# Projection bias on GpSimd, matmul operands on two byte phases, and new engine orders

## The chip, the cores and the metric

The kernel runs on one core of one Trainium2 chip. The metric is device time in microseconds (us). One execution was also taken by the hardware profiler. TensorE is PE in the rows (PEld is its weight load), VectorE is DVE, ScalarE is ACT, GpSimd is POOL, and SP is the engine that issues the DMAs.

## The reference

Two layers on x of shape (2, 1024, 256), all in float32, cut to what matters here:

```python
# layer 0: cross attention to a context of 154 rows, a router over 3 experts, a gate
nx = layer_norm(x)
weights = softmax(nx @ Wq @ (context @ Wk).T / 16)           # one head
evidence = weights @ (context @ Wv)
combined = concat([nx, evidence, anchor])                      # anchor: cond, the same in every row
probs = softmax(combined @ router_W + router_b)
routed = sum_e probs[e] * (silu(combined @ e_w1[e] + e_b1[e]) @ e_w2[e] + e_b2[e])
g = sigmoid(silu(combined @ gate_w1 + gate_b1) @ gate_w2 + gate_b2)
x = x + g * (routed @ out_w + out_b)
# layer 1: cross attention with 16 heads of 16 to the same context, modulated by cond
xq, xkv = ada_ln(x, cond), ada_ln(context, cond)
q, k, v = xq @ Wq + bq, split(xkv @ Wkv + bkv)
out = softmax(q @ k.T / 4) @ v                                  # per head
return x + (out @ Wp + bp)                                      # bp: the bias that the change moves
```

## The kernel before

The 2048 tokens are cut into 8 tiles `t` of 256 (two halves `s` of 128). `LAST` is tile 7 and `NEXT` is tile 6. Each engine's work is written out by hand as a list of steps in `ORDERS`, and each engine goes through its own list in order; a step is `name.tile.part`. A step waits on semaphores for the steps of other engines that it needs. TensorE's list has 545 steps.

A float32 product is made of three float32r matmuls (helper `exact`, L1658 to L1660): high by high, low by high, high by low. In `mm(out, left, right)`, `left` is the stationary operand (loaded with LDWEIGHTS) and `right` is the moving one. The steps on TensorE that matter here:

- `za.t.u` and `z.t.u` (`hidden_half`, L1658 to L1660 and L1878): the two halves of hidden unit `u` (7 units a tile: the gate's first layer and the three experts' in slices of 256). 13 matmuls a half: the stationary operands are the weights WNh, WNl, VWh, VWl, VWD (`hidden_w_*`, `context_w_*`), the moving ones NXh, NXl, PTh, PTl, PTD (`normed_*`, `probs_T_*`). Over the kernel that is 8 x 7 x 2 x 13 = 1,456 matmuls.
- `p.t.u` (`second`): the second layer of unit `u`. 12 matmuls: stationary SH and SL (`hidden_high`, `hidden_low`), moving W2h, W2l, GWh, GWl (`expert_out_*`, `gate_out_*`). Over the kernel 8 x 7 x 12 = 672. SH is made by ScalarE (L1023) and SL by GpSimd (step `h`, L1592).
- `query.t`: 12 matmuls, stationary `query_w_*`, moving `query_in_*`. `most` (L1997) and `score` (L2027): attention scores, with `query_stack` and `pair_keys`, whose column offsets differ from step to step. `value` (L2050, L2053): in four column groups of 32.
- `proj.t` (`proj_part`; for the last tile `lead.7`, `last.0`, `last.1`): for each half `s`, four matmuls L2061 (stationary `outs_low`, moving `proj_w_high`), two L2065 (`outs_pairs`, `proj_w_low`) and, behind the first of them, one L2063 (`bias_rows` by `second_bias`) that adds bp, which is kept as a high and a low row in `second_bias`.
- `cv.0`, `warm.0`, `ck.0`, `cv.1`, `fold.0`: the start. `cv.0` waits for the first DMA; `warm.0` is 4 matmuls on zeros (8 rows in the trace) and waits only for a memset on VectorE. `fill` are matmuls on data that nobody reads, between the waits at the end.

VectorE subtracts the projection's PSUM bank from the token tile X (`proj`, `last_add`), and SP stores X. X has 5 slots, with a reload for later tiles. `xhat.t` on ScalarE reads X for the second layer norm.

SBUF places are given out by `put`, one after the other, each size rounded up to 32 bytes; `run` lays overlays on top of places given out before. No place is aligned to more than that.

Of the kernel before, what the change touches and what calls it, by code (L numbers as in the profile page):

```python
# [89 lines left out]
def packed(np, v):  # L90
# [35 lines left out]
    gate_rows[[1, 17]] = v["L1_xcond_bp"]  # L126
# [138 lines left out]
        most.1.14 z.3.0 za.3.1 most.1.15 vw.1.0 z.3.1 vw.1.1 row.1.0 p.2.5 p.2.6 proj.0 za.3.2 z.3.2 vw.1.2 score.1.0 p.3.0 qx.2 score.1.1 za.3.4 score.1.2
        score.1.3 za.3.3 score.1.4 score.1.5 score.1.6 query.2 z.3.3 score.1.7 value.1.0 value.1.1 att.4 score.1.8 score.1.9 z.3.4 most.2.0 most.2.1 p.3.1
        most.2.2 score.1.10 p.3.2 za.3.5 most.2.3 most.2.4 score.1.11 value.1.2 value.1.3 most.2.5 most.2.6 z.3.5 most.2.7 most.2.8 za.3.6 prob.4 most.2.9
        most.2.10 z.3.6 p.3.3 vw.1.3 most.2.11 p.3.4 za.4.0 most.2.12 most.2.13 vw.1.4 z.4.0 za.4.1 most.2.14 z.4.1 most.2.15 vw.1.5 p.3.5 row.2.0 p.3.6
        vw.1.6 za.4.2 z.4.2 norm.5 p.4.0 proj.1 score.2.0 za.4.3 qx.3 z.4.3 score.2.1 score.2.2 score.2.3 p.4.1 score.2.4 query.3 score.2.5 score.2.6
        score.2.7 value.2.0 value.2.1 score.2.8 score.2.9 att.5 score.2.10 score.2.11 value.2.2 most.3.0 most.3.1 value.2.3 most.3.2 most.3.3 za.4.4 most.3.4  # L270
        za.4.5 z.4.4 most.3.5 most.3.6 p.4.2 prob.5 z.4.5 most.3.7 most.3.8 p.4.3 za.4.6 most.3.9 z.4.6 p.4.4 za.5.0 most.3.10 most.3.11 z.5.0 za.5.1 p.4.5
        most.3.12 p.4.6 za.5.2 most.3.13 most.3.14 most.3.15 z.5.1 z.5.2 row.3.0 norm.6 proj.2 p.5.0 za.5.3 qx.4 score.3.0 score.3.1 z.5.3 score.3.2 score.3.3
        score.3.4 query.4 score.3.5 score.3.6 score.3.7 value.3.0 value.3.1 score.3.8 att.6 score.3.9 za.5.4 p.5.1 score.3.10 p.5.2 most.4.0 score.3.11
        most.4.1 za.5.5 most.4.2 most.4.3 most.4.4 z.5.4 most.4.5 most.4.6 value.3.2 value.3.3 most.4.7 most.4.8 za.5.6 most.4.9 most.4.10 prob.6 z.5.5
        most.4.11 most.4.12 p.5.3 most.4.13 most.4.14 z.5.6 most.4.15 p.5.4 za.6.0 z.6.0 row.4.0 za.6.1 norm.7 z.6.1 p.5.5 p.5.6 proj.3 score.4.0 score.4.1
        score.4.2 p.6.0 score.4.3 score.4.4 score.4.5 za.6.2 score.4.6 za.6.3 qx.5 score.4.7 value.4.0 value.4.1 score.4.8 query.5 score.4.9 score.4.10 z.6.2
        z.6.3 score.4.11 att.7 value.4.2 value.4.3 most.5.0 most.5.1 most.5.2 p.6.1 za.6.4 most.5.3 z.6.4 most.5.4 most.5.5 za.6.5 most.5.6 most.5.7 p.6.2
        most.5.8 prob.7 most.5.9 z.6.5 most.5.10 za.6.6 most.5.11 p.6.3 z.6.6 p.6.4 most.5.12 most.5.13 most.5.14 za.7.0 z.7.0 p.6.5 p.6.6 most.5.15 za.7.1
        za.7.2 z.7.1 row.5.0 z.7.2 p.7.0 za.7.3 qx.6 proj.4 score.5.0 score.5.1 score.5.2 query.6 score.5.3 score.5.4 z.7.3 score.5.5 p.7.1 value.5.0
        score.5.6 score.5.7 score.5.8 value.5.1 score.5.9 score.5.10 most.6.0 p.7.2 most.6.1 score.5.11 most.6.2 value.5.2 most.6.3 most.6.4 most.6.5  # L280
        value.5.3 most.6.6 most.6.7 most.6.8 za.7.4 most.6.9 most.6.10 z.7.4 most.6.11 za.7.5 p.7.3 za.7.6 z.7.5 z.7.6 most.6.12 most.6.13 most.6.14 p.7.4
        most.6.15 row.6.0 p.7.5 p.7.6 proj.5 score.6.0 score.6.1 fill.0 score.6.2 score.6.3 fill.1 score.6.4 fill.2 score.6.5 score.6.6 value.6.0 score.6.7
        qx.7 score.6.8 value.6.1 score.6.9 query.7 score.6.10 value.6.2 score.6.11 most.7.0 most.7.1 most.7.2 most.7.3 most.7.4 most.7.5 most.7.6 most.7.7
        most.7.8 most.7.9 most.7.10 most.7.11 most.7.12 most.7.13 row.7.0 value.6.3 most.7.14 most.7.15 score.7.0 score.7.1 score.7.2 score.7.3 score.7.4
# [57 lines left out]
        load.0 late.0 late.1 key.0 key.1 stack.0.0 stack.0.1 stack.0.2 stack.0.3 row.0.0 stack.1.0 again.0 stack.1.1 stack.1.2 stack.1.3 again.1 again.2  # L342
        row.1.0 proj.0 again.3 reload.0 stack.2.0 stack.2.1 stack.2.2 stack.2.3 again.4 again.5 again.6 row.2.0 proj.1 reload.1 stack.3.0 stack.3.1 stack.3.2
        stack.3.3 row.3.0 proj.2 reload.2 stack.4.0 stack.4.1 stack.4.2 stack.4.3 row.4.0 stack.5.0 stack.5.1 proj.3 stack.5.2 stack.5.3 row.5.0 stack.6.0
        stack.6.1 stack.6.2 proj.4 stack.6.3 unstack.0 row.6.0 stack.7.0 proj.5 stack.7.1 stack.7.2 stack.7.3 proj.6 last.0 last.1
# [1776 lines left out]
```

## Time and profile before

| what | value |
|---|---|
| median of 3 runs | 431.21 us (428.57, 431.21, 814.35) |
| the profiled execution | 429.68 us, of which the span of its instructions is 427.9 us |
| TensorE busy | 416.2 us (97%) |
| VectorE, ScalarE, GpSimd busy | 327.5, 225.6, 171.2 us (77, 53, 40%) |

[...] What a matmul costs in a stream is the distance from its start to the next start, here called its pitch. It is read from the timeline, whose starts are given to 0.01 us: over a long stretch without a wait, the difference of two starts divided by the number of matmuls.

### The profile page before, as it was taken

What the parts mean: (1) busy time and instruction counts of PE and PEld (TensorE: products, weight loads), DVE (VectorE), ACT (ScalarE), POOL (GpSimd) and SP (SyncE); (2) the same over time, 40 slices, a digit from 0 to 9 for tenths busy, and PEclk for the clock granted to TensorE, in tenths of its full rate; (3) what the DMA queues carried; (4) which work ended last, traced back from release to release, by engine and by line L of the source; (5) the groups of instructions that cost most, each with busy time, mean ns of one, the idle gap of its engine ahead of it and who ended that gap; (6) DMA issues with size and microseconds to landing.
All of it is one profiled execution on the core that took longest, in us unless ns stands there. A gap on an engine that the chain in (4) does not pass through costs nothing.

```text
span 427.9 us, 9498 instructions
## 1 busy us (share of the span) xinstructions
PE 416.2 (97%) x3541; PEld 382.9 (89%) x3541; DVE 327.5 (77%) x780; ACT 225.6 (53%) x495; POOL 171.2 (40%) x183
## 2 busy tenths in 40 slices
PE   6999989999999999999999999999999999999997
PEld 5787889899999889998999899989998998887866
DVE  1697686783876579859985799789849987994897
ACT  1887822516445644476348643862683358337272
POOL 1348484724622263225611725165315435332110
PEclk9999998999999999999999999999999999999999
DMA  8747440421300220032201300130003001410401
GB/s 293 233 157 276 173 147 2 92 57 45 70 1 5 63 64 6 23 100 51 72 7 51 75 1 2 55 75 2 3 14 88 2 4 32 106 26 2 100 2 49
DMA packets 16981, 28.06 MB, mean 66 GB/s; under 512 B 3816, under 2 KB 9128, under 8 KB 16936
## 3 DMA queue, kind: packets, MB, share of 16 engines
q1 hardware_dynamic: 16808, 27.45, 22.2%
q8 instruction: 28, 0.46, 0.5%
q14 instruction: 17, 0.14, 0.1%
q10 hardware_dynamic: 128, 0.01, 0.0%
HBM read 16.20 MB, written 2.10 MB: 43 GB/s over the span
## 4 chain that ended last, share of the span: by engine, by line
PE 87%; DVE 6%; ACT 4%; issue 2%; DMA 1%; DVEq 0%; ACTq 0%
PE hidden_banks L1658 9%; PE hidden_banks L1659 9%; PE hidden_banks L1660 9%; PE token_bank L1658 6%; PE token_bank L1659 6%; PE token_bank L1660 6%; PE score_banks L1665 5%; PE score_banks L2027 5%; PE score_banks L1997 4%; PE value_bank L2050 3%; PE hidden_banks L1878 3%; PE value_bank L2053 3%; PE value_bank L1665 3%; PE head_bank L1665 2%; PE value_bank L2061 1%
## 5 line engine op out<-in xcount | busy, mean ns | idle before, releaser
L1592 POOL TENSOR_TENSOR hidden_low<-hidden,hidden_high 128x512 fp32r<-128x512 f32 x56 | 72.9, 1302 | 139.3 <-ACT hidden_high L1023 139.2
L1015 ACT ACTIVATE hidden<-hidden_banks 128x512 f32<-128x512 f32 x56 | 33.3, 599 | 64.2 <-PE hidden_banks L1878 64.1
L1658 PE MATMUL hidden_banks<-normed_high,hidden_w_high 128*128 128x256 f32 x224 | 66.1, 295 | 0.8 <-DVE hidden L1348 0.8
L1431 DVE TENSOR_REDUCE head_maxima<-score_banks 128x2 f32<-128x308 f32 x128 | 56.5, 473 | 11.0 <-PE score_banks L1997 9.3
L1083 ACT ACTIVATE exp_ring<-score_banks 128x512 f32<-128x512 f32 x96 | 53.3, 604 | 21.0 <-PE score_banks L2027 17.6
L1659 PE MATMUL hidden_banks<-normed_high,hidden_w_low 128*128 128x256 f32 x224 | 63.3, 283 | 0.0
L1660 PE MATMUL hidden_banks<-normed_low,hidden_w_high 128*128 128x256 f32 x224 | 63.3, 283 | 0.0
L1658 PE MATMUL token_bank<-expert_out_high,hidden_high 128*128 128x256 f32 x192 | 55.2, 288 | 0.5 <-DVE expert_sum L1385 0.5
L1659 PE MATMUL token_bank<-expert_out_high,hidden_low 128*128 128x256 f32 x192 | 54.3, 283 | 0.0
L1660 PE MATMUL token_bank<-expert_out_low,hidden_high 128*128 128x256 f32 x192 | 54.1, 282 | 0.0
L1023 ACT CAST hidden_high<-hidden 128x512 fp32r<-128x512 f32 x56 | 34.7, 619 | 24.2 <-PE token_bank L1660 13.4
L1658 PEld LDWEIGHTS hidden_banks<-normed_high,hidden_w_high 128*128 128x128 f32 x224 | 42.5, 190 | 2.2 <-issue 1.8
L1348 DVE SCALAR_TENSOR_TENSOR hidden<-hidden,hidden_banks 128x512 f32<-128x512 f32 x56 | 37.8, 678 | 8.3 <-ACT hidden L1015 8.0
L1659 PEld LDWEIGHTS hidden_banks<-normed_high,hidden_w_low 128*128 128x128 f32 x224 | 42.7, 191 | 0.2
L1660 PEld LDWEIGHTS hidden_banks<-normed_low,hidden_w_high 128*128 128x128 f32 x224 | 42.6, 190 | 0.0
L1658 PEld LDWEIGHTS token_bank<-expert_out_high,hidden_high 128*128 128x128 f32 x192 | 36.6, 190 | 1.0 <-ACT hidden_high L1023 0.7
L1659 PEld LDWEIGHTS token_bank<-expert_out_high,hidden_low 128*128 128x128 f32 x192 | 36.7, 191 | 0.1
L1660 PEld LDWEIGHTS token_bank<-expert_out_low,hidden_high 128*128 128x128 f32 x192 | 36.7, 191 | 0.0
L1505 POOL TENSOR_TENSOR rstd<-mean_var,minus_half 128x2 f32<-128x2 f32 x18 | 14.3, 797 | 46.0 <-DVE mean_var L1124 45.9
L1878 PE MATMUL hidden_banks<-probs_T_tail,context_w_tail 100*128 100x256 f32 x112 | 31.8, 284 | 0.0
L1660 PE MATMUL hidden_banks<-probs_T_low,context_w_high 128*128 128x256 f32 x112 | 31.8, 284 | 0.0
L1659 PE MATMUL hidden_banks<-probs_T_high,context_w_low 128*128 128x256 f32 x112 | 31.8, 284 | 0.0
(288 smaller groups left out, 1133.5 us busy)
## 6 DMA issues: line engine op xcount, KB each, us to landing
unit_weights<-units SPq DMA_DIRECT2D x7, 768.0 KB, 5.2
query_stack<-queries_high SPq DMA_DIRECT2D x56, 64.0 KB, 2.0
tokens<-x SPq DMA_DIRECT2D x8, 256.0 KB, 4.8
query_stack<-queries_low SPq DMA_DIRECT2D x28, 64.0 KB, 2.0
w_slice<-units SPq DMA_DIRECT2D x7, 256.0 KB, 2.8
out<-tokens SPq DMA_DIRECT2D x7, 256.0 KB, 2.2
w_T<-folds SPq DMA_DIRECT2D x6, 256.0 KB, 4.9
pair_keys<-keys_high SPq DMA_DIRECT2D x16, 77.0 KB
```

The source lines that it names most:

```text
L1015: nc.scalar.activation(TB[:, ring(t, u), :], Z[:, hidden_bank(t, u), :], ACT.Tanh, scale=0.5).then_inc(scalar_z, 1)
L1023: nc.scalar.copy(SH[:, ring(t, u), :], TB[:, ring(t, u), :]).then_inc(scalar_h, 1)
L1083: nc.scalar.activation(E[:, w % ERING, :], S[:, ring_of[key][0], :], ACT.Exp).then_inc(scalar_score, 1)
L1348: v.scalar_tensor_tensor(out=TB[:, ring(t, u), :], in0=TB[:, ring(t, u), :], scalar=1.0, in1=Z[:, hidden_bank(t, u), :], op0=ALU.add, op1= ...
L1431: v.tensor_reduce(MX[:, s, first:first + step + 1:step], S[:, ring_of[key][0], 0:2 * CTX].rearrange("p (j n) -> p j n", j=2), AX.X, ALU.ma ...
L1592: nc.gpsimd.tensor_tensor(SL[:, ring(t, u), :], TB[:, ring(t, u), :], raw(SH[:, ring(t, u), :]), ALU.subtract).then_inc(gpsimd_h, 1)
L1658: mm(out_, lh, rh, start=start, stop=False, skip_group_check=skip)
L1659: mm(out_, ll, rh, start=False, stop=False, skip_group_check=skip)
L1660: return mm(out_, lh, rl, start=False, stop=stop, skip_group_check=skip)
L1665: last = mm(out_, l, r, start=(i == 0), stop=(i == len(pairs) - 1))
L1878: return mm(half, VWD[0:BROWS, b, c], PTD[0:BROWS, t % 2, :], start=False, stop=True)
L2027: last = mm(bank, left, QS[:, c, :], start=True, stop=True)
```

## The change

The `proj` matmul L2063 is gone. bp is loaded by a DMA as 128 equal rows (`BP`), and a new GpSimd step `bias.t` adds it to X after `xhat.t` has read X; `proj` and `last_add` on VectorE wait for it. A new `begin(phase)` moves the allocator to the next address with that remainder modulo 256, and the operands are put in a new sequence: W2, GW and NX, PT begin at 0; the hidden weights (with the query and projection weights behind them), the hidden tiles SH, SL, and the region R1 with query operands, `query_stack` and projection operands begin at 64. The four lists in `ORDERS` are rewritten; TensorE's list has the same 545 steps in another order, GpSimd's gains the 8 `bias` steps.

```diff
+LINE = 256
+STREAMED = 64
...
-    gate_rows[[1, 17]] = v["L1_xcond_bp"]
...
+"proj_b": v["L1_xcond_bp"],
...
 "tensor":
-        cv.0 warm.0 ck.0 cv.1 fold.0 vw.0.0 norm.0 vt.0 att.0 vt.1 vr.0 vt.2 prob.0 ...
+        warm.0 cv.0 ck.0 cv.1 fold.0 vr.0 vw.0.0 norm.0 vt.0 vt.1 att.0 vw.0.1 vt.2 ...
...
-        fill.7 fill.8 fill.9 fill.10 proj.6 fill.11 fill.12 lead.7 last.0 fill.13 last.1
+        value.7.0 score.7.5 score.7.6 score.7.7 value.7.1 score.7.8 score.7.9 score.7.10 value.7.2 score.7.11 value.7.3 fill.3 proj.6 fill.4 fill.5 fill.6
+        fill.7 fill.8 fill.9 lead.7 last.0 fill.10 last.1 fill.11 fill.12 fill.13
...
 "gpsimd":
+        ... norm.2 h.1.0 qn.0 h.1.1 bias.0 h.1.2 low.2 ...
+        ... h.7.2 zero.0 sum.5.0 bias.5 sum.5.1 h.7.3 h.7.4 h.7.5 h.7.6 sel.0 qn.7 sum.6.0 sum.6.1 bias.6 sum.7.0 bias.7 sum.7.1
...
+        def begin(phase):
+            at[0] += (phase - at[0]) % LINE
+            return at[0]
...
-        weights_at = at[0]
+        experts_at = begin(0)
+        W2h = put("expert_out_high", [P, 2 * (NU - 1), D], F32R)
+        W2l = put("expert_out_low", [P, 2 * (NU - 1), D], F32R)
+        GWh = put("gate_out_high", [P, KC, D], F32R)
+        GWl = put("gate_out_low", [P, KC, D], F32R)
+        weights_at = begin(STREAMED)
         WNh = put("hidden_w_high", [P, KC, ZCOLS], F32R)
...
-        hidden_at = at[0]
+        begin(0)
+        NXh = put("normed_high", [P, 2, KC, TILE], F32R)
+        NXl = put("normed_low", [P, 2, KC, TILE], F32R)
+        PTh = put("probs_T_high", [P, 2, TILE], F32R)
+        PTl = put("probs_T_low", [P, 2, TILE], F32R)
+        PTD = put("probs_T_tail", [P, 2, TILE], F32R)
+        hidden_at = begin(STREAMED)
         TB = put("hidden", [P, 2, 512])
...
         SH = put("hidden_high", [P, 2, 512], F32R)
         SL = put("hidden_low", [P, 2, 512], F32R)
...
-        R1 = at[0]
+        R1 = begin(STREAMED)
...
+                sp.dma_start(BP[:, :], a["proj_b"].partition_broadcast(P)).then_inc(proj_b_loaded, 16)
...
             def last_add(key):
                 dve.wait_ge(tensor_last, upto(tensor_last, key, "o"))
+                dve.wait_ge(gpsimd_bias, upto(gpsimd_bias, ("bias", LAST), "x"))
...
             def proj(key):
                 dve.wait_ge(tensor_proj, upto(tensor_proj, key, "o"))
+                dve.wait_ge(gpsimd_bias, upto(gpsimd_bias, key_of("bias", key), "x"))
...
+            def bias(key):
+                t = key[1]
+                pool.wait_ge(scalar_xhat, upto(scalar_xhat, ("xhat", t), "xh"))
+                pool.wait_ge(proj_b_loaded, 16)
+                nc.gpsimd.tensor_tensor(X[:, t % SLOTS, :, :], X[:, t % SLOTS, :, :],
+                                        BP[:, :].unsqueeze(1).to_broadcast([P, NSUB, D]), ALU.add).then_inc(gpsimd_bias, 1)
...
             def proj_part(t, s, groups):
                 for g in groups:
                     mm(proj_bank(t, s), both[:, g, c], WPh[:, g, :], start=(g == 0), stop=False)
-                    if g == 0:
-                        mm(proj_bank(t, s), BSEL[:, 1 + EXPERTS:2 + EXPERTS].to_broadcast([P, P]), CB[:, :], start=False, stop=False)
-                    elif g % 2:
+                    if g % 2:
                         last = mm(proj_bank(t, s), pairs[:, g // 2, c], WPl[:, g // 2, :], start=False, stop=(g == GROUPS - 1))
```

The new DMA of `BP` stands behind that of `value_bias_row`, ahead of the `late.0` step, which loads the projection's weights. In SP's list a few `again`, `row` and `proj` steps change places.

## Rows read from the trace of the kernel before

**Rows 1.** The page, part 1: busy time, share of the span, instructions.

```profile
PE 416.2 (97%) x3541; PEld 382.9 (89%) x3541; DVE 327.5 (77%) x780; ACT 225.6 (53%) x495; POOL 171.2 (40%) x183
```

**Rows 2.** Waits of PE: us in total, times, longest us.

```profile
PE score_banks L1665 <- DMA context_and_value_w<-first: 4.2, 1, 4.2
PE score_banks L1806 <- DVE router_const L1187: 1.2, 1, 1.2
PE hidden_banks L1658 <- DVE hidden L1348: 0.8, 1, 0.8
...
PE score_banks L2027 <- ACT exp_ring L1083: 0.2, 1, 0.2
```

**Rows 3.** PE's timeline (start us, duration us): inside a `z`, operands on equal phases.

```profile
176.57 0.28 PE L1658 MATMUL hidden_banks<-normed_high,hidden_w_high 128*128 128x256 f32 x1
...
178.37 0.28 PE L1660 MATMUL hidden_banks<-probs_T_low,context_w_high 128*128 128x256 f32 x1
```

**Rows 4.** Timeline of PE and PEld: a `p` (equal phases), two scores, then the `query` of tile 3.

```profile
230.29 0.28 PE L1658 MATMUL token_bank<-expert_out_high,hidden_high 128*128 128x256 f32 x1
230.29 0.19 PEld L1659 LDWEIGHTS token_bank<-expert_out_high,hidden_low 128*128 128x128 f32 x1
...
231.60 0.28 PE L1660 MATMUL token_bank<-expert_out_low,hidden_high 128*128 128x256 f32 x1
...
231.96 0.28 PE L1658 MATMUL head_bank<-query_in_high,query_w_high 128*128 128x256 f32 x1
...
233.26 0.28 PE L1660 MATMUL head_bank<-query_in_low,query_w_high 128*128 128x256 f32 x1
```

**Rows 5.** PE's timeline: the `query` of tile 4.

```profile
273.04 0.28 PE L1659 MATMUL head_bank<-query_in_high,query_w_low 128*128 128x256 f32 x1
...
274.17 0.28 PE L1660 MATMUL head_bank<-query_in_low,query_w_high 128*128 128x256 f32 x1
```

**Rows 6.** PE's timeline: the projection of tile 0, second half, to the next step.

```profile
175.50 0.28 PE L2063 MATMUL value_bank<-second_bias,bias_rows 128*128 128x256 f32 x1
175.62 0.28 PE L2061 MATMUL value_bank<-proj_w_high,outs_low 128*128 128x256 f32 x1
175.74 0.29 PE L2065 MATMUL value_bank<-proj_w_low,outs_pairs 128*128 128x256 f32 x1
175.87 0.39 PE L2061 MATMUL value_bank<-proj_w_high,outs_low 128*128 128x256 f32 x2
176.10 0.28 PE L2065 MATMUL value_bank<-proj_w_low,outs_pairs 128*128 128x256 f32 x1
176.21 0.28 PE L1658 MATMUL hidden_banks<-normed_high,hidden_w_high 128*128 128x256 f32 x1
```

**Rows 7.** POOL by line and form (busy us, mean ns; idle before), and two of its waits.

```profile
L1592 POOL TENSOR_TENSOR hidden_low<-hidden,hidden_high 128x512 fp32r<-128x512 f32 x56 | 72.9, 1302 | 139.3 <-ACT hidden_high L1023 139.2
POOL hidden_low L1592 <- ACT hidden_high L1023: 139.2, 41, 8.2
POOL last_sums L1638 <- ACT last_outs_and_sums L1093: 5.3, 1, 5.3
```

**Rows 8.** Timeline of the first microseconds.

```profile
0.90 0.43 DVE L1132 MEMSET probs<- 128x448 f32 x1 [0.90 <-PEq L2113]
4.21 2.42 PE L1665 MATMUL score_banks<-context_and_value_w 128*128 128x154 f32 x8 [4.21 <-DMA context_and_value_w<-first]
6.43 3.23 PE L1678 MATMUL hidden_banks<-probs 128*128 128x256 f32 x8
9.50 1.21 PE L1665 MATMUL score_banks<-context_and_value_w,context_and_key_w 128*128 128x154 f32 x8
11.59 1.21 PE L1665 MATMUL score_banks<-keys_T,query_score_w_raw 128*128 128x154 f32 x8
```

**Rows 9.** DMA issues: count, KB each, us from issue to landing; SP's issue of two.

```profile
unit_weights<-units SPq DMA_DIRECT2D x7, 768.0 KB, 5.2
query_score_w_raw<-query_score_w SPq DMA_DIRECT2D x1, 256.0 KB, 6.0
value_bias_row<-value_b SPq DMA_DIRECT2D x1, 128.0 KB, 8.9
2.59 0.47 SPq L749 DMA_DIRECT2D query_score_w_raw<-query_score_w  x1
```

**Rows 10.** Stretches: us, busy PE PEld DVE ACT POOL (instructions), PEclk, DMA share, GB/s.

```profile
5.00:10.00 5.00, 5.00 (x19) 4.41 (x18) 1.26 (x6) 0.00 (x0) 1.22 (x2) 1.00 1.03 387
150.00:200.00 50.00, 50.00 (x452) 46.68 (x454) 39.62 (x93) 27.87 (x61) 18.71 (x17) 1.00 0.18 48
200.00:250.00 50.00, 50.00 (x437) 46.56 (x430) 40.14 (x101) 26.71 (x59) 22.65 (x24) 1.00 0.18 48
250.00:300.00 50.00, 50.00 (x446) 47.68 (x445) 43.71 (x101) 25.34 (x55) 22.82 (x20) 1.00 0.11 29
```

More of the change, by code:

```diff
@@ L265 @@
[L265 to L284, printed above, removed]
@@ L304 @@
[L304 to L306 removed]
+        setup.0 ck.0 cv.0 silu.0 cv.1 fold.0 unit.0 vw.0.0 norm.0 vt.0 vt.1 att.0 vt.2 low.0 route.0 vw.0.1 unit.1 gsplit.0 vw.0.2 unit.2 z.0.0 vt.3 vw.0.3
@@ L330 @@
-        most.7.13 most.7.14 most.7.15 dup.6.0 sums.6.0 row.7.1 out.6.0 dup.7.0 sums.7.0 outl.6.0 out.7.0 dup.7.1 sums.7.1 out.7.1 outl.7.0 outl.7.1 proj.6
+        setup.0 bias1.0 ln.0 fold.0 group.0 vw.0.0 vr.0 vt.0 att.0 vt.1 prob.0 vt.2 route.0 silu.0 vw.0.1 cb.0 vt.3 vw.0.2 z.0.0 vw.0.3 ln.1 vt.4 share.0 w2.1
+        logit.0 vw.0.4 w2.2 vt.5 vw.0.5 z.0.1 vw.0.6 att.1 mod.0 mod.1 z.0.2 prob.1 mod.2 vt.6 mod.3 z.0.3 keyn.0 share.1 fold.1 w2.3 keyn.1 z.0.4 ln.2 bq.0
+        route.1 w2.4 key.0 evac.0.1 w2.5 logit.1 z.0.5 w2.6 z.0.6 evac.0.2 key.1 evac.0.3 z.1.0 res.0 qn.0 shift.0 z.1.1 z.1.2 qlow.0 query.0 z.1.3 att.2 ln.3
@@ new lines @@
+        most.5.1 share.7 prob.7 most.5.2 z.6.4 most.5.3 dup.4.0 most.5.4 most.5.5 most.5.6 most.5.7 evac.6.1 sums.4.0 most.5.8 z.6.5 most.5.9 route.7
+        most.5.10 z.6.6 most.5.11 evac.6.2 most.5.12 out.4.0 z.7.0 most.5.13 most.5.14 evac.6.3 most.5.15 res.6 qn.6 row.5.0 z.7.1 shift.6 outl.4.0 qlow.6
+        logit.7 proj.4 query.6 z.7.2 init.7 z.7.3 most.6.0 most.6.1 most.6.2 most.6.3 most.6.4 evac.7.1 most.6.5 most.6.6 most.6.7 most.6.8 most.6.9 dup.5.0
+        sums.5.0 z.7.4 most.6.10 out.5.0 most.6.11 z.7.5 most.6.12 most.6.13 z.7.6 most.6.14 most.6.15 evac.7.2 row.6.0 outl.5.0 evac.7.3 res.7 qn.7 proj.5
@@ L331 @@
+        shift.7 qlow.7 query.7 most.7.0 most.7.1 most.7.2 most.7.3 most.7.4 most.7.5 most.7.6 most.7.7 most.7.8 most.7.9 most.7.10 most.7.11 row.7.0 most.7.12
+        most.7.13 dup.6.0 most.7.14 most.7.15 sums.6.0 row.7.1 out.6.0 dup.7.0 sums.7.0 outl.6.0 out.7.0 dup.7.1 sums.7.1 out.7.1 outl.7.0 outl.7.1 proj.6
         last.0 last.1
@@ L340 @@
     """,
     "sync": """
[L342 to L345, printed above, removed]
+        load.0 late.0 late.1 key.0 key.1 stack.0.0 stack.0.1 stack.0.2 stack.0.3 again.0 again.1 row.0.0 stack.1.0 stack.1.1 stack.1.2 stack.1.3 row.1.0
```

152 lines of the change are left out of this document (79 added, 73 removed).

## The prediction, made before the changed kernel was run

> **What bounds the kernel now.** I read the page's busy shares first, then PE's list of waits, then PE's own timeline. The shares say which engine to look at: PE is busy 97% of the span and the next engine 77% [rows 1]. That share alone could hide waits inside overlapping matmuls, so the waits come second: beside 4.2 us at the start for the first DMA, the nine others run from 1.2 to 0.2 us, in all 4.6 us of 427.9 [rows 2]. So there is almost no wait to remove. PE's stream itself is the time, and there are two ways to shorten it: fewer matmuls, or a shorter pitch. The timeline gives the pitch, and here the reader should compare stretches. Inside a `z`, 15 matmuls take 178.37 - 176.57 = 1.80 us, 120.0 ns each [rows 3]. A `p` of 12 gives 11 steps in 231.60 - 230.29 = 1.31 us, 119.1 ns [rows 4]. The `query` just behind it, with the same three lines, shape and type, takes 1.30 us for 11 steps, 118.2 ns [rows 4], and the `query` of tile 4 takes 274.17 - 273.04 = 1.13 us for 10 steps, 113.0 ns [rows 5]. [...]
>
> **What differs is the byte phase.** [...] I work the places out from the allocator. All sizes from `hidden_w_high` to `proj_w_low` are multiples of 256 bytes, and from `score_w` up to `hidden` the places add up to 50,944 = 199 x 256, so in `z` and `p` all operands stand on one and the same remainder modulo 256. From `x_hat0` to R1 it is 7,744 = 30 x 256 + 64, so the moving operand of `query` stands 64 above the stationary one (weights minus moving = -64), and in `proj`, where the stationary `outs_*` are in R1, it is the other way (+64). The `proj` rows show what +64 does: behind the bias matmul, whose operands are on equal phases again, the starts are 0.12, 0.13 apart, and then three matmuls take 176.21 - 175.87 = 0.34 us, 113 ns [rows 6]. So a stream on +64 goes to 113 ns after some five matmuls. `query` on -64 runs at it in one tile [rows 5] and stays at 118 in another [rows 4].
>
> **The change, part by part.** Working total: the profiled execution, 429.7 us (427.9 of span and 1.8 around it), 1.5 under the median of the runs, 431.2. Minus means gain.
>
> *Phases, `z` and `p`.* After the change the moving NX, PT, W2 and GW are at 0 and the stationary weights and SH, SL at 64: +64 for all 1,456 + 672 = 2,128 matmuls, also where a `z` passes to a `p` and back. In the new order of TensorE these come in 107 unbroken runs; counting the first five of each run as not yet settled gives 535, and 1,593 settled. Against 119.4 ns now (between 120.0 and 119.1), the settled ones at 113.5 save 5.9 ns each, 1,593 x 5.9 = -9.4 us; the first five at 117.5 save 535 x 1.9 = -1.0 us. Sum -10.4. Ends: if all stay at 118.2, as `query` in rows 4, 2,128 x 1.2 = -2.6; if all are at 113.0, 2,128 x 6.4 = -13.6; below nothing, the single step of 0.13 us with weights 64 ahead [rows 6] bounds it (a rival, below). I take -10.4, because the rows with the same sign as the new places settle at 113.
>
> [...]
>
> *Phases, the rest.* `query` and `proj` weights come to 64 too, and so do their partners in R1: equal phases, where they had 64 between them. 96 `query` matmuls at +2 ns and 72 of `proj` (tiles 0 to 5, without the bias) at +3.5 ns are 0.19 + 0.25, about +0.5 us. `most` and `score` had changing offsets and keep them: 0. Ends 0 to +1 (168 x 6).
>
> *The bias matmul.* 2 a tile, 8 tiles: 16 at 0.12 us [rows 6], all in PE's stream: -1.9 us.
>
> *GpSimd's add.* 8 additions of 128x512. The nearest row is `hidden_low`, same size, two inputs, 1302 ns [rows 7]: 8 x 1.3 = 10.4 us on an engine busy 40%. What is queued behind it is mostly `h`, which `p` waits for. But GpSimd waits 139.2 us in 41 waits for ScalarE ahead of those [rows 7], 3.4 us each, so 1.3 us fits in. At the end `bias.7` stands ahead of `sum.7.1`, where GpSimd waited 5.3 us [rows 7]. Cost 0; without the cover at most 10.4 us. VectorE's new wait in `proj` and `last_add` is for a step that needs only `xhat` of the same tile, which lies before that tile's scores: 0. In the last tile the stores would be behind it, and the wait for `bias.7` would have to be longer than the whole of `sum`, `out` and `last`.
>
> *The DMA of bp.* One more issue of 128 KB behind `value_bias_row` (8.9 us to landing for the same size [rows 9]), long before the first projection. SP's next step, `late.0`, waits for setup steps anyway. Cost 0; uncovered, about half a microsecond (0.47 for an issue [rows 9]).
>
> *The start.* `warm.0` takes 9.50 - 6.43 = 3.1 us between `cv.0` and `ck.0` [rows 8]. It needs only a memset that ends at 0.90 + 0.43 = 1.3 us, while PE idles to 4.21 [rows 2, 8]; ahead of `cv.0` it runs from 1.4 to 4.5, and some 2.8 of its 3.1 us fall in that idle time. What is late next: `fold.0` (now at 11.59) needs the score weights, issued at 2.59 and landed 6.0 later, at 8.6 [rows 8, 9], and the copy of `ck.0`'s result. That allows at most 11.6 - 8.6 = 3.0 us. `cv.0` runs at twice the time of `ck.0` for the same form (2.42 against 1.21 us [rows 8]), after no work on PE; I leave that as it is. In the first 10 us DMA is full (share 1.03 [rows 10]), and units of 768 KB follow, so the gain can also be eaten by a later landing. Ends 0 and -3.0; I take -2.2, nearer to the landing of the score weights.
>
> *The orders.* At best they remove the 4.6 us of PE's waits [rows 2]; at worst they add as much. I take 0. But a faster PE meets the others sooner: in 250 to 300 us DVE is busy 43.71 of 50 [rows 10], and that sum doesn't shrink. Estimate: a third more of the 4.6 us, +1.5.
>
> Sum: -10.4 + 0.5 - 1.9 - 2.2 + 1.5 = -12.5; 429.7 - 12.5 = 417.2 us.
>
> **The rivals.**
> 1. *Settles at 118, not 113.* The streams of `z` are not `proj`; seven equal steps may not be enough evidence, and rows 4 show 64 bytes between at 118.2 for a whole `query`. Then -2.6 in place of -10.4, and +0.5 given back in place of 1.5: 429.7 - 2.6 + 0.5 - 1.9 - 2.2 + 0.5 = 424.0.
> 2. *The phase does nothing.* What makes 113 would be the moment at which loads and matmuls lock, by chance: the two `query` streams [rows 4, 5] have the same addresses and differ by 5 ns. Against it: the `z` and `p` rows don't show 113. 429.7 - 1.9 - 2.2 = 425.6. [...]
> 3. *VectorE takes over.* With DVE at 43.71 of a stage that would shrink to 48.3 us [rows 10], 90% busy, its chains (`most`, `evac`, `query`) may hold PE. If half of the phase gain is lost: 417.2 + 5.2 = 422.4.
> 4. *Slower: the step of 0.13 us.* With weights 64 ahead, one matmul in the second half of `proj` takes 0.13 us [rows 6], more than any in `z`. If that is what +64 does outside short groups, at 124 ns, 2,128 x 4.6 = +9.8: 429.7 + 9.8 + 0.5 - 1.9 - 2.2 = 435.9. It decides against the change from a mean pitch of some 121 ns (119.4 + 3.6 / 2.128). Against it: the 0.13 stands between 0.12 and a stretch at 113, as a step of the settling.
>
> **How the numbers follow.** Chances: forecast 0.60, rival 1 0.20, rival 3 0.07, rival 2 0.08, rival 4 0.05. The predicted time is the forecast's, 417.2. Its own range, with the ends -13.6 of the phases, 0 to -3.0 of the start and an order that gives or takes 3, is about 411 to 422. The range for 8 in 10 reaches on to rivals 3, 1 and 2: 411 to 425.5. Two per cent, about what can be told from no change in this kernel, is 8.6 us of 431.2: faster begins under 422.6, slower over 439.8. The forecast lies under 422.6 nearly always (0.57), rival 3 in half of its cases (0.04), rival 1 with a good start and order in a third (0.07): 0.68 faster. Rival 4 ends at 436, over 439.8 only with a bad order, so slower is 0.03, and the rest, 0.29, is within 2%.
>
> **What would show it.** Right: in the timeline after, 13 and more `z` matmuls in a row at 113 to 114 ns, the mean durations of L1658 to L1660 down by as much as the pitch; `query` at 119 to 120; no L2063; `warm.0` before 4 us and `fold.0` by about 9.4; a POOL row of 128x512 x8 near 1.3 us with nobody waiting for it. Wrong: `z` at 117 to 118 (rival 1) or 119 to 120 (rival 2); pitch as forecast, but PE's waits grown to 6 us and more behind DVE or ACT (rival 3); `z` at 124 (rival 4). A wait of `p` for `hidden_low`, or of `fold.0` or the first `vw` for a DMA, would take back single terms.

## The result, and the profile after

The changed kernel took 423.8 us (median of 4 runs, 423.2 to 425.5) beside 429.9 for the kernel before on the same chip: a ratio of 0.9875, with an interval of 0.984 to 0.991. The 429.9 counts in an execution of 814 us that the ratio leaves out. That is a gain of 1.25%, some 5.4 us and less than half of the forecast's 12.5, under the bound of 2%. The profiled execution has a span of 421.4 us, where before had 427.9.

A correction first: a half of a hidden unit is 10 matmuls, not the 13 that the text ahead of the prediction and the prediction say: three times three of 128 rows and one of 100. The stretch of [rows 3] holds one of these last in the middle, among the rows that are left out there:

```profile
177.29 0.28 PE L1878 MATMUL hidden_banks<-probs_T_tail,context_w_tail 100*128 100x256 f32 x1
```

So `z` has 8 x 7 x 2 x 10 = 1,120 matmuls, and with the 672 of `p` the phases work on 1,792, not 2,128.

The busy shares (part 1 of the page after) answer to [rows 1]: 16 instructions fewer on PE, eight more on POOL, PE as full as before.

```profile
PE 410.3 (97%) x3525; PEld 374.3 (89%) x3525; DVE 325.3 (77%) x780; ACT 225.6 (54%) x495; POOL 181.1 (43%) x191
```

PE's waits after answer to [rows 2] (engine, line, releaser: us, times, longest):

```profile
PE head_bank L1866 <- POOL x_hat L1617: 1.7, 1, 1.7
PE head_bank L1887 <- POOL probs L1630: 1.6, 1, 1.6
PE hidden_banks L1698 <- DVE values_T L1146: 1.4, 1, 1.4
PE hidden_banks L2081 <- DVE last_outs_pairs L1488: 1.3, 2, 1.1
PE value_bank L2070 <- ACT exp_ring L1094: 1.2, 1, 1.2
PE value_bank L1685 <- DVE context_w_tail L1219: 0.8, 1, 0.8
```

The 1.4 us is the short wait of `warm.0` that stands where 4.2 stood. The others, with five from 0.6 to 0.2, add up to 8.4 us; they were 4.6. PE's timeline answers to [rows 3 to 6]: two `p` (24 matmuls), a `proj` (12), a half of a `z`, and in another place the `query` of tile 3.

```profile
164.54 0.28 PE L1678 MATMUL token_bank<-expert_out_high,hidden_high 128*128 128x256 f32 x1
...
164.89 0.28 PE L1678 MATMUL token_bank<-expert_out_high,hidden_high 128*128 128x256 f32 x1
...
167.16 0.28 PE L1680 MATMUL token_bank<-expert_out_low,hidden_high 128*128 128x256 f32 x1
167.27 0.39 PE L2081 MATMUL value_bank<-proj_w_high,outs_low 128*128 128x256 f32 x2
...
168.69 0.41 PE L2047 MATMUL score_banks<-query_stack,pair_keys 100*128 100x256 f32 x2
168.94 0.28 PE L1678 MATMUL hidden_banks<-normed_high,hidden_w_high 128*128 128x256 f32 x1
...
169.98 0.28 PE L1898 MATMUL hidden_banks<-probs_T_tail,context_w_tail 100*128 100x256 f32 x1
...
222.87 0.28 PE L1678 MATMUL head_bank<-query_in_high,query_w_high 128*128 128x256 f32 x1
...
224.17 0.28 PE L1680 MATMUL head_bank<-query_in_low,query_w_high 128*128 128x256 f32 x1
```

In `p` the first three steps take 0.35 us (117 ns), the next 20 take 2.27 us: 113.5 ns. The 12 of `proj` take 1.42 us, 118 ns. The `z` has 9 steps in 1.04 us, 115.6 ns. The `query` has 11 in 1.30, 118.2. So the settled pitch is the forecast one, but a `z` is too short to be in it for long. Over the whole kernel I take the distance from each start to the next and leave out the steps of 135 ns and more (waits and changes of shape; some 1,085 of 1,120 and 660 of 672 remain): `z` goes from 119.6 to 116.1 ns, `p` from 119.4 to 115.6.

By place in a `z`, the mean steps after are 120.3, 118.4, 116.4, 115.4, 114.7, 114.6, 114.4, 114.6, 114.5 and, for the 100-row matmul L1898, 118.6. In the mean, then, a `z` starts again at 120. By what stands straight before it: behind another half of a `z`, and so behind its 100-row matmul, the first step is 120.8 ns (30 of them), behind a `p`, all of 128 rows and at the same distance, 115.3 (only 7).

The start, from PE's timeline after, answers to [rows 8]:

```profile
1.38 3.78 PE L1698 MATMUL hidden_banks<-probs 128*128 128x256 f32 x8 [1.38 <-DVE values_T L1146]
...
9.35 1.21 PE L1685 MATMUL score_banks<-keys_T,query_score_w_raw 128*128 128x154 f32 x8
...
11.16 1.84 PE L1685 MATMUL score_banks<-values_T,constants 128*128 128x154 f32 x12 [0.25 <-DVE router_const L1198]
...
13.69 0.60 PE L1866 MATMUL head_bank<-constants,x_hat 128*128 128x128 f32 x4
...
16.09 1.34 PE L1685 MATMUL head_bank<-score_w,normed 128*128 128x157 f32 x8
...
21.95 0.33 PE L1887 MATMUL head_bank<-constants,probs 128*128 128x128 f32 x1 [1.60 <-POOL probs L1630]
...
25.43 0.38 PE L1678 MATMUL hidden_banks<-normed_high,hidden_w_high 128*128 128x256 f32 x1
```

`fold.0` starts at 9.35 for 11.59: 2.2 us earlier, as forecast. But the first `z` starts at 25.43, where it started at 25.45 before. `vr.0` (11.16) now stands ahead of `norm.0` (13.69), and what hangs on `norm.0`, that is `att.0` (16.09), the softmax and `prob.0` (21.95), comes no earlier; PE waits 1.6 us for it.

On GpSimd (lines by form, then the line L1617, its own timeline and VectorE's at 254 us, and PE's next row), the new addition is there as forecast [rows 7], and one of the waits above is explained:

```profile
L1605 POOL TENSOR_TENSOR hidden_low<-hidden,hidden_high 128x512 fp32r<-128x512 f32 x56 | 72.9, 1305 | 135.1 <-ACT hidden_high L1034 135.1
L1662 POOL TENSOR_TENSOR tokens<-tokens,proj_bias 128x512 f32<-128x512 f32 x8 | 10.3, 1286 | 0.0
L1617 POOL TENSOR_SCALAR x_hat<-tokens,mean_var,rstd x16: 1220/1228/2987, 8.7 to 289.7; 128x256 f32<-128x256 f32 x16
254.00 4.56 POOL L1617 TENSOR_SCALAR x_hat<-tokens,mean_var,rstd 128x256 f32<-128x256 f32 x2
253.95 1.26 DVE L1486 SCALAR_TENSOR_TENSOR outs_low<-outs_high,constants,outs_twice 128x1024 fp32r<-128x1024 f32 x1
258.62 0.66 PE L1866 MATMUL head_bank<-constants,x_hat 128*128 128x128 f32 x4 [1.71 <-POOL x_hat L1617]
```

The addition takes 1286 ns and nobody waits for it. `x_hat` takes 1228 ns in the median (min/median/max in its row), but the pair for `norm.6` took 4.56 us beside VectorE's work, and the new list has PE at `norm.6` before it is done.

### The profile page after: what moved, and what is told of

The parts are those of the page before. It is cut to its first block, busy times and chain, and to the rows that moved or that the text cites. A ratio compares the mean times of both kernels' runs of the same rounds, so it can differ in the third digit from the quotient of the medians.

```text
span 421.4 us, 9492 instructions
## 1 busy us (share of the span) xinstructions
PE 410.3 (97%) x3525; PEld 374.3 (89%) x3525; DVE 325.3 (77%) x780; ACT 225.6 (54%) x495; POOL 181.1 (43%) x191
## 4 chain that ended last, share of the span: by engine, by line
PE 88%; DVE 4%; POOL 3%; ACT 3%; issue 2%; ACTq 0%; POOLq 0%; DVEq 0%
PE hidden_banks L1678 9%; PE hidden_banks L1679 9%; PE hidden_banks L1680 9%; PE score_banks L1685 7%; PE token_bank L1678 6%; PE token_bank L1679 6%; PE token_bank L1680 6%; PE score_banks L2047 5%; PE score_banks L2017 4%; PE value_bank L2070 4%; PE hidden_banks L1898 3%; PE value_bank L2073 3%; PE value_bank L1685 3%; PE head_bank L1685 2%; PE value_bank L2081 1%
## 5 line engine op out<-in xcount | busy, mean ns | idle before, releaser
L1680 PE MATMUL hidden_banks<-normed_low,hidden_w_high 128*128 128x256 f32 x224 | 62.3, 278 | 0.0
L1679 PE MATMUL token_bank<-expert_out_high,hidden_low 128*128 128x256 f32 x192 | 53.4, 278 | 0.0
L1679 PEld LDWEIGHTS hidden_banks<-normed_high,hidden_w_low 128*128 128x128 f32 x224 | 42.4, 189 | 0.2
L1898 PE MATMUL hidden_banks<-probs_T_tail,context_w_tail 100*128 100x256 f32 x112 | 31.5, 281 | 0.0
L1678 PE MATMUL hidden_banks<-probs_T_high,context_w_high 128*128 128x256 f32 x112 | 31.1, 277 | 0.0
```

The source lines that it names most:

```text
L1678: mm(out_, lh, rh, start=start, stop=False, skip_group_check=skip)
L1679: mm(out_, ll, rh, start=False, stop=False, skip_group_check=skip)
L1680: return mm(out_, lh, rl, start=False, stop=stop, skip_group_check=skip)
L1898: return mm(half, VWD[0:BROWS, b, c], PTD[0:BROWS, t % 2, :], start=False, stop=True)
```

## The experiments

Each is timed against the kernel before on the same chip; pitches are means as above.

| run | what it is | median us | ratio to before, interval | `z`, `p` ns |
|---|---|---|---|---|
| (changed kernel) | all | 423.8 | 0.9875, 0.984 to 0.991 | 116.1, 115.6 |
| e1 | before + places | 424.4 | 0.9888, 0.986 to 0.992 | 116.0, 115.8 |
| e2 | before + orders | 430.1 | 1.0029, 1.0005 to 1.005 | 119.6, 119.4 |
| e3 | before + bias on GpSimd | 429.0 | 0.9983, 0.996 to 1.001 | 119.6, 119.4 |
| e4 | changed, distance 0 | 429.7 | 1.0028, 1.0003 to 1.005 | 119.6, 119.5 |
| e5 | changed, distance 192 | 426.8 | 0.9942, 0.992 to 0.997 | 117.8, 117.2 |
| e6 | changed, `setup2.0` late | 425.3 | 0.9901, 0.987 to 0.993 | 115.9, 115.4 |
| e7 | changed, tail on 128 rows | 425.7 | 0.9907, 0.987 to 0.994 | 115.2, 115.0 |
| e9 | changed, old lists | 423.5 | 0.9851, 0.982 to 0.988 | 116.0, 115.6 |
| e10 | changed, old start | 424.0 | 0.9870, 0.983 to 0.991 | 116.1, 115.5 |
| e11 | changed, `query`, `proj` at 64 | 425.8 | 0.9898, 0.986 to 0.994 | 116.1, 115.5 |
| e12 | places, bias, old lists, e7, e11 | 421.5 | 0.9799, 0.977 to 0.983 | 115.7, 115.3 |
| e13 | changed, `norm.6` later | 424.1 | 0.9858, 0.982 to 0.990 | 116.0, 115.5 |
| e14 | e7, e10, e11, e13 together | 423.8 | 0.9851, 0.981 to 0.989 | 115.6, 115.2 |

**The three parts alone.** e1 takes the `begin` lines and the new sequence of `put` into the kernel before, e2 the four lists, e3 the addition on GpSimd, its DMA and its waits.

> The kernel before, with only the new places of the operands (bias matmul and orders as before). Theory A, the pitch: z and p settle at 113 ns inside each step but start each step near 120, so their mean falls from 119.4 to about 116 ns and the time by 1,792 x 3.5 ns = 6 us (ratio 0.986). Rival B, other engines: PE's shorter stream is eaten by waits for VectorE and ScalarE, so the pitch falls but the time by 2 us or less (0.995 or more). Rival C, locking by chance: pitch unchanged at 119 to 120 and ratio 1.000.

> The kernel before, with only the four new lists of steps (the bias steps of GpSimd are skipped, the bias matmul stays, the places stay). Theory A: the new orders bring nothing or cost 1 to 2 us: the start gains 2 us at the first fold and gives it back by the first hidden unit; ratio 1.000 to 1.005. Rival B: the orders are what gains, ratio 0.990 to 0.993, with the pitch at 119.4.

> The kernel before, with only the bias moved to GpSimd (8 steps put into its old list at about the new list's places). Theory A: 16 matmuls less at 0.117 us, -1.9 us, ratio 0.996, no wait of PE for GpSimd. Rival: the additions delay the low halves of the hidden tiles and PE waits for them, ratio 1.000 or above.

The places alone give nearly the whole result, and move the pitch of the same matmuls in the same order by 3.6 ns: address does it. The orders alone cost 0.3%. The bias alone gives 0.2%, an interval that takes in none at all, though 16 matmuls are gone.

**Distance 0 and distance 192.**

```diff
-STREAMED = 64
+STREAMED = 0      # e4
+STREAMED = 192    # e5, with head_maxima and router_probs moved into the gap
```

> The changed kernel with the second remainder set to 0 as well, so that all operands of z and p are on equal phases again; all else as changed. Theory A: z and p at 119.4 ns again, 6 us above the changed kernel, ratio 1.000 (0.997 to 1.003) to the kernel before. Rival B: 2 us or less above the changed kernel, ratio 0.988 to 0.993.

> The changed kernel with the second remainder 192 in place of 64: in z and p the weights stand 64 bytes below the moving operand (-64) and not above; all else as changed but for two small tiles moved into a gap. If the sign matters, as the query rows of the kernel before suggest (118 in seven of eight, 113 in one), z and p run at 117 to 118 ns, 3 us above the changed kernel (ratio 0.994 to 0.996). Rival: any distance of 64 settles at 113 to 114 ns, ratio as the changed kernel, 0.987.

PE's timeline of a `z`, first e4 and then e5:

```profile
163.56 0.28 PE L1678 MATMUL hidden_banks<-normed_high,hidden_w_high 128*128 128x256 f32 x1
...
164.64 0.28 PE L1898 MATMUL hidden_banks<-probs_T_tail,context_w_tail 100*128 100x256 f32 x1
```

```profile
162.18 0.28 PE L1678 MATMUL hidden_banks<-normed_high,hidden_w_high 128*128 128x256 f32 x1
...
163.24 0.28 PE L1898 MATMUL hidden_banks<-probs_T_tail,context_w_tail 100*128 100x256 f32 x1
```

Nine steps in 1.08 us are 120.0 ns, in 1.06 us 117.8. At distance 0 the changed kernel is no faster than before, so all that it gains net comes from the places: between e4 and the changed kernel the ratios differ by 1.5%, some 6.5 us, and the pitches by 1,120 x 3.5 + 672 x 3.9 = 6.5 us. At 192 it has 1.8 ns of the 3.5. Both size and sign of the distance count.

**What throws a `z` back to 120.** In e7 the tail has 128 rows, the rest of them zeros:

```diff
-        mm(half, VWD[0:BROWS, b, c], PTD[0:BROWS, t % 2, :], start=False, stop=True)
+        mm(half, VWD[0:P, b, c], PTD[0:P, t % 2, :], start=False, stop=True)
```

> The changed kernel with the last matmul of each half hidden unit on 128 rows in place of 100, the added rows being zeros (a memset more on VectorE at the start). Theory: the load of other than 128 rows is what throws the stream out of its 113 ns; then that matmul falls from 118.6 to 114 ns and a half unit that follows at once starts at 114 in place of 120; z from 116.1 to about 115 ns in the mean, 1 to 1.5 us in all. Rival: every new step starts at 120 whatever stands before it (another PSUM bank, a semaphore), and the pitches stay as they are.

The tail's own step falls from 118.6 to 115.1, the mean first step of a `z` from 120.3 to 118.1, the mean to 115.2: about 0.85 x 1,120 + 0.55 x 672 = 1.3 us. The first step splits as the theory said, and against its rival: straight behind another half it falls from 120.8 to 114.7 (30 in each trace), behind steps of other kinds than `z` and `p` it stays at 121 (44 in each). So it is the other row count, and not a new step as such. The total doesn't show the gain. In this execution the load of the score weights landed 6.8 us after its issue, for 4.6 in the profile of the changed kernel; PE stood for it, and then the granted clock fell (a row of e7's timeline, and two of its windows: us, busy PE PEld DVE ACT POOL, granted clock, DMA share, GB/s):

```profile
9.53 1.28 PE L1686 MATMUL score_banks<-keys_T,query_score_w_raw 128*128 128x154 f32 x8 [1.46 <-DMA query_score_w_raw<-query_score_w]
10.00:20.00 10.00, 9.75 (x75) 8.13 (x73) 4.68 (x16) 5.05 (x12) 7.80 (x25) 0.83 0.73 215
20.00:30.00 10.00, 7.63 (x55) 4.45 (x55) 8.21 (x18) 7.79 (x21) 5.49 (x6) 0.83 0.22 76
```

The first `z` starts at 28.8 us for 25.4. From there to the end it is 395.3 us for 395.9 in the changed kernel, with a clock of 1.00 from 30 us on in both: about half of the 1.3 us shows.

e8 is a kernel of its own: streams of equal 128x256 matmuls on operands of ones, with the weights at eight distances from the moving operand (its output is zeros).

> No layer is computed here: the output is zeros, and the kernel only runs TensorE streams of 40 equal matmuls (128 rows, 256 columns, float32r, data all ones) for eight distances of the weights above the moving operand, 0 to 224 bytes in steps of 32; then eight times nine matmuls of 128 rows and one of 100, at 0 and at 64; then the same with ten of 128 rows. Theory: 119 to 120 ns at 0, 113 to 114 at 64, 113 to 118 at 192, and at 64 the matmul of 100 rows throws the stream out for some four matmuls. Rival, lock by chance: the pitch in a stream doesn't go by the distance.

The granted clock is 1.00 up to 95 us, where the streams end. Per distance of 40 matmuls, first start to last over 39 steps: 120.0 ns at 0, 118.3 at 32, 117.8 at 64, 117.3 at 96, 118.6 at 128, 119.8 at 160, 117.8 at 192, 116.8 at 224. Then nine matmuls and one of 100 rows, again and again, at 0 and at 64; then 80 and 80 without (L68):

```profile
57.10 1.23 PE L63 MATMUL bank<-moving,weights_bytes 128*128 128x256 f32 x9
58.17 0.28 PE L64 MATMUL bank<-moving,weights_bytes 100*128 100x256 f32 x1
58.29 1.24 PE L63 MATMUL bank<-moving,weights_bytes 128*128 128x256 f32 x9
...
67.84 1.20 PE L63 MATMUL bank<-moving,weights_bytes 128*128 128x256 f32 x9
68.88 0.28 PE L64 MATMUL bank<-moving,weights_bytes 100*128 100x256 f32 x1
69.00 1.20 PE L63 MATMUL bank<-moving,weights_bytes 128*128 128x256 f32 x9
...
75.92 19.18 PE L68 MATMUL bank<-moving,weights_bytes 128*128 128x256 f32 x160
```

At 0 ten take 1.20 us, but for the rounding of the starts, at 64 1.16. Step by step the ten at 64 are 121, 119, 116, 114, 113, 113, 114, 113, 113, 117 ns: a `z` of the kernel, without the kernel. And the plain stream at 64 never leaves 117 to 119 (117.8 in the mean, 80 matmuls). So 64 has two pitches at the same addresses. What sends a stream into one or the other is not isolated: here each of the eight stretches with a 100-row matmul in every ten goes to 113, and each of the two streams without (40 and 80 matmuls) stays at 118. `query`, at 192, may have shown both in the same way [rows 4, 5]; in e2 and e3, at the same addresses, that of tile 4 took 118 ns, not 113.

**Where the start's 2.2 us went.** e6 moves GpSimd's memsets (`setup2.0`), beside which VectorE's small copies took 3.0, 2.0 and 1.9 us, back behind `norm.1`; e10 gives the lists the start of before, `warm.0` still first.

```diff
-        ln.0 norm.0 unit.0 setup2.0 prob.0 ...                                     # gpsimd, e6 and e10
+        ln.0 norm.0 unit.0 prob.0 ... ln.1 norm.1 setup2.0 ...
-        warm.0 cv.0 ck.0 cv.1 fold.0 vr.0 vw.0.0 norm.0 vt.0 vt.1 att.0 ...        # tensor, e10
+        warm.0 cv.0 ck.0 cv.1 fold.0 vw.0.0 norm.0 vt.0 att.0 vt.1 vr.0 ...
```

> The changed kernel with one step of GpSimd's list, setup2.0 (memsets and small copies), back behind norm.1, where the old list has it about. Theory: in the new list it runs beside three VectorE instructions of the start that take 3.0, 2.0 and 1.9 us, and delays norm.0's and prob.0's work on GpSimd, and so eats the 2.2 us that the first fold gained; then the first hidden unit comes 1.5 to 2.5 us earlier (25.4 to about 23.5 us) and the ratio is 0.982 to 0.984. Rival: the start is held by the landing of the unit weights, first hidden unit at 25 us, ratio 0.987.

> The changed kernel with the start of its lists put back to the sequence of the kernel before, as far as the first z, but with warm.0 still first; setup2.0 back behind norm.1. Theory A (the chain norm, att, softmax, prob sets the start, and the new lists put vr and vw ahead of norm and so gave the 2.2 us back): norm.0 starts at about 11.8 instead of 13.69, att.0 at 13.5 instead of 16.09, the first z at 23.3 to 23.6 instead of 25.43; total 422 if the lead is kept, ratio 0.983. Theory B (a load, or VectorE's and ScalarE's work on the unit weights, holds the first z): norm.0 earlier by as much, but the first z within 0.5 us of 25.4, with PE waiting longer for a copy or a load; total 423 to 424.

e6 left the first `z` at 25.3: the memsets don't hold it. In e10 (PE's timeline) everything comes as the chain allows:

```profile
11.36 0.60 PE L1865 MATMUL head_bank<-constants,x_hat 128*128 128x128 f32 x4
...
13.07 1.34 PE L1684 MATMUL head_bank<-score_w,normed 128*128 128x157 f32 x8
...
22.86 0.36 PE L1677 MATMUL hidden_banks<-normed_high,hidden_w_high 128*128 128x256 f32 x1
```

The first `z` starts 2.6 us earlier, even a little more than theory A had. 1.6 us of it goes again at 29 us, where PE waits for `second_bias` of VectorE, and some 0.9 stays to the end: span 420.4 for 421.4. The medians (424.0 and 423.8) don't tell the two apart.

**The orders.** e9 is the changed kernel with the lists of before, `bias` steps put in; e13 moves one step of the new lists.

```diff
-        ... za.5.2 z.5.1 norm.6 proj.2 score.3.0 score.3.1 score.3.2 z.5.2 score.3.3 ...     # tensor, e13; scalar likewise
+        ... za.5.2 z.5.1 proj.2 score.3.0 score.3.1 score.3.2 z.5.2 norm.6 score.3.3 ...
```

> The changed kernel with the four lists of the kernel before; only the eight bias steps are put into GpSimd's list, each behind a hidden step of about the place that it has in the new list. Theory A (the new lists give nothing on PE and cost a good microsecond, as they did alone): the pitch stays at 116.1 and 115.7 ns, PE's waits fall back by 2 to 4 us, total 1.0 to 1.5 us under the changed kernel, ratio to before about 0.985. Theory B (the shorter stream needs the new lists, because the others' work has to come earlier): PE's waits grow further beside those of the changed kernel, total 425 or more, ratio 0.989 or more.

> The changed kernel with one step moved: norm.6 goes behind z.5.2 in TensorE's list (it stood ahead of proj.2) and behind score.3.2 in ScalarE's. Theory A (the new lists put this step where x_hat of GpSimd, 4.6 us beside VectorE's work, isn't ready, and PE simply stands): the wait of 1.7 us for x_hat is gone, z.6 starts 1.3 to 1.7 us earlier against z.5, total 1.3 to 1.7 us under the changed kernel. Theory B (VectorE and ScalarE set the pace of this stage, PE is only early): the wait comes back within 10 us under another name (exp_ring, hidden_low or head_maxima), z.6 at the same distance from z.5 as before, total the same.

e9 is at least as fast as the changed kernel, although its PE stands until 4.2 us again: the new lists are worth nothing with the new places either. In e13 the wait for `x_hat` is gone and doesn't come back under another name. From tile 5's first `z` to tile 6's it is 42.4 us, for 43.9 in the changed kernel: 1.4 won. Its total hides that, and here PE was busy without a gap when the granted clock fell (windows of e13):

```profile
50.00:55.00 5.00, 5.00 (x34) 5.00 (x33) 3.65 (x11) 3.13 (x6) 4.91 (x6) 0.71 0.00 0
55.00:60.00 5.00, 5.00 (x28) 4.98 (x27) 3.26 (x10) 0.96 (x3) 4.03 (x4) 0.61 0.74 262
```

Between tile 0's first `z` and tile 1's this execution loses 3.3 us to the changed kernel, whose clock was 1.00 there. That is what the two rows give: 5 x (1 - 0.71) + 5 x (1 - 0.61) = 3.4 us.

**`query` and `proj`, and all together.** In e11 `proj_w_*` stand at 0 and `query_w_*` at 128, so that the stationary operand is 64 above the moving one there too. e12 has this, e7's tail, the places and the bias, with the lists of before (only `warm.0` first); e14 the same with the new lists, e10's start and e13's step.

```diff
+        WPh = put("proj_w_high", [P, GROUPS, D], F32R)               # ahead of the hidden weights, at 0
+        WPl = put("proj_w_low", [P, GROUPS // 2, D], F32R)
         weights_at = begin(STREAMED)
...
+        begin(2 * STREAMED)
         WQh = put("query_w_high", [P, KC, D], F32R)
```

> The changed kernel with the projection weights put to remainder 0 and the query weights to 128, so that in query and proj too the stationary operand stands 64 above the moving one. Theory A (the sign and size of the distance set the pitch of any stream): query from 119.1 to about 115.5, proj from 118.8 to about 116, z and p as in the changed kernel; 192 matmuls by some 3.3 ns are 0.6 us, ratio 0.986. Rival (groups of 12 and 6 matmuls are too short to settle): 118 in both, 0.2 us, nothing that can be told.

> Phases and bias on GpSimd with the lists of the kernel before (only warm.0 first), the tail matmul of z on 128 rows, and query and proj on a distance of 64 as well. If the single results add (orders 1.2 us, tail 1.3, query and proj 0.6): about 420.5 us, ratio 0.979; if the lists of before hold the first z no longer, up to 2 us less. If the shorter stream only turns into waits of PE for VectorE and ScalarE: 423 to 424, with PE's waits over 9 us.

> The changed kernel with the start of the kernel before (warm.0 first), norm.6 later, the tail matmul on 128 rows, and query and proj at a distance of 64. If the single gains add (start 1.0, norm.6 1.5, tail 1.3, query and proj 0.5) and no fall of the clock takes them: 419.5 us, ratio 0.975. If the stages behind give back what is gained, as the start did: 421 to 422, like the earlier combination.

The projection of e11, PE's timeline:

```profile
170.37 0.39 PE L2082 MATMUL value_bank<-proj_w_high,outs_low 128*128 128x256 f32 x2
...
171.73 0.40 PE L2048 MATMUL score_banks<-query_stack,pair_keys 100*128 100x256 f32 x2
```

12 steps in 1.36 us, 113.3 ns; over the kernel `proj` goes from 118.8 to 115.4 and `query` from 119.1 to 116.8, which is 0.5 us. The timing doesn't show it: in the profiled execution the score weights landed after 6.5 us, and the clock was 0.83 from 10 to 30 us; and from the first `z` to the end it is 396.3 us for the changed kernel's 395.9, with a new wait of 0.4 us for `query_stack`. So the pitch of `query` and `proj` goes with the distance, but a gain in time is not shown. e12 is the fastest by interval: 0.980, below the changed kernel, with the bound of 2% inside it (0.977 to 0.983), so that it isn't shown to pass that; its best times are 420.1 and 420.2, where the changed kernel's best is 423.2. Its profiled execution, from which its pitches come, was its longest (426.4). e14 comes as low only in its best run (420.3); in its profile the clock was 0.78 and 0.54 at 50 to 60 us, which by the same sum is 3.4 us of 423.9.

## Why the prediction was wrong in size

**The phases: right in kind, 3.9 us too large.** The step that failed is the working of -10.4. First the count: the 336 too many were all among the settled ones, 336 x 5.9 = 2.0 us. Second the settling, the other 1.9: I let a stream settle once in each of 107 unbroken runs. The places in a `z`, e7 and e8 show that a 100-row matmul throws it out, so a `z` behind another settles anew. Instead of a mean of 114.5 (the forecast's 535 at 117.5 and 1,593 at 113.5) it came to 116.1 and 115.6, together 1,120 x 3.5 + 672 x 3.8 = 6.5 us. The matmuls at 113 in rows 5 and 6 stand in steps without a 100-row one, and I read over the one in the stretch of rows 3; I didn't ask what the other row count in the stream does. The granted clock was 1.00 in all the stretches that the prediction compares [rows 10], so it doesn't make the difference of 120 and 113 ns. e1 and e4 show that address alone makes this gain: 3.6 ns a matmul with the places alone, and 119.6 and 119.5 ns again at distance 0. Why it does is not shown. The trace has the next load beside each matmul (a matmul from 230.29 for 0.28 us, the next one's load from 230.29 for 0.19 [rows 4]), but not when either reads its operand.

**`query` and `proj`: right.** 119.1 and 118.8 after, 117.4 and 116.9 before: +0.3 of the +0.5.

**The bias: right on PE, not in time.** 16 matmuls at 0.12 are gone, GpSimd's addition takes 1.29 us and is waited for by nobody. Alone (e3) it gave 0.8 us of span and nothing that the interval can tell from zero, not 1.9.

**The start: -2.2 at `fold.0`, 0 at the first `z`.** This is the second step that failed. I asked what is late next and stopped at a load; late was the chain from `norm.0` through `att.0` and the softmax to `prob.0`, ahead of which the new lists put other work. e10 shows it: same loads, `norm.0` 2.3 us earlier, first `z` 2.6 us earlier. The later landing that the prediction named as the danger came too: the score weights took 6.7, 6.7, 6.8 and 6.5 us from issue to landing in e4, e5, e7 and e11, for 4.6 in the changed kernel.

**The orders and what is given back: 0 and +1.5 forecast.** The spans differ by -6.5 us, but not all of that is the kernel's: the profile of before has a fall of the granted clock that the changed kernel's has not (two windows of before; in the changed kernel the clock in them is 1.00).

```profile
60.00:65.00 5.00, 3.76 (x25) 3.39 (x25) 4.90 (x15) 3.08 (x9) 2.19 (x2) 0.88 0.55 198
65.00:70.00 5.00, 5.00 (x23) 4.40 (x23) 1.51 (x6) 2.17 (x4) 0.00 (x0) 0.78 0.02 3
```

By these rows it cost an estimated 5 x 0.12 + 5 x 0.22 = 1.7 us, which leaves -4.8. The phases, `query` and `proj`, and bias are -6.5 + 0.3 - 1.9 = -8.1. Three of the `fill` groups (12 matmuls, 1.4 us) now stand behind the last projection, off the path. So some +4.7 is given back behind the first `z`, where +1.5 was forecast. Of this the waits listed there explain 1.5 (5.7 us for 4.2): `x_hat` 1.7, `last_outs_pairs` 1.0 more, `exp_ring` 0.8 more, against two that went. The new lists also let a `z` follow a step of another shape more often: its steps of 135 ns and more, without the waits and the fall, are 35 for 25, and what they take above 120 ns each is 4.1 us in all for 2.8. And `most` takes 19.2 us from start to start for 18.3, as it does in e2. The `x_hat` part is shown (e13); the others are read from one trace each, and about 1 us is not assigned. e2 and e9 agree that the lists cost and don't give. The waits grew past the 6 us that I named as the mark of rival 3, and one of them does lie beside VectorE's work; for that one VectorE isn't the bound, since one moved step won it back. The other waits weren't tested, so a part of the 4.7 may still be rival 3's.

**The rivals.** Rival 1's 424.0 is the measured time, but its mechanism is not: long stretches settle at 113.5. Its pitch exists (117.8 ns in e8's plain stream at 64, 117.8 and 117.2 in e5). Rival 2 falls as the whole account with e1 and e4; rival 4 falls with the mean of 116.

## What to carry to other kernels

Where TensorE's stream is the time, read the pitch in the timeline and try the distance between the stationary and the moving operand modulo 256 (no run here tries another modulus); it was worth 3.5 ns of 120 here. Count a stream's matmuls from the rows, with every odd shape in it, before multiplying a pitch. Look at the granted clock of each stretch before two spans are subtracted: here an estimated 1.7 of 6.5 us were the clock's. And a step that comes earlier helps only as far as the chain behind it: name the chain up to the next large block, not the next load alone.
